# Edge scatter in float32r parts, the loop written out, and new instruction lists for five engines

## The chip, the core and the metric

The kernel runs on one core of a Trainium2 chip. Its engines are TensorE (matmuls and transposes, PE in the profile, with its weight loads as PEld), VectorE (DVE), ScalarE (ACT), GpSimd (POOL) and SyncE (SP), which here issues nearly all DMAs. Each engine runs its own list of instructions in order and waits on semaphores for the others. The metric is the device time of one execution in microseconds; lower is better.

## What is computed

x has 16 batches of 512 nodes by 128 features. Four graph layers follow each other, all within one launch. Layer 0 is eight Euler steps over the adjacency; layer 1 a graph attention with a residual; layer 2 (the "edge" stage) an attention over 256 listed edges; layer 3 a Chebyshev step ("cheb"), a four-head attention of 512 nodes with a mask ("att"), and a feed-forward block with layer norms ("ffn"). The part that the change touches in its arithmetic is the end of the edge layer:

```python
Vt = Xv[:, dst].transpose(1, 0, 2, 3)
Y = jax.ops.segment_sum(attn[..., None] * Vt, src, num_segments=n)
Y = Y.transpose(1, 0, 2, 3).reshape(bt, n, d)
return Y @ W_out.T
```

In the kernel the segment sum is a matmul: U (the 256 edges' weighted values, edges on partitions) times src_rows, a table of zeros and ones with a one where an edge starts at a node.

## The kernel before

`build_front` computes layer 0 for all batches, the tables, and the first two layers' steps for batch 0 and part of batch 1; it ends near 405 us. `build_layers` then runs the other stages as a pipeline over batches. A stage has a lag: `gat` 0, `edge` 1, `cheb` 2, `att` 3, `ffn` 4. `ORDER` (line 1858) holds a list of steps for each engine; in turn i of the loop a step of lag L works on batch i - L, and each "+" behind its name adds one to the lag. `FILL_ORDER` and `DRAIN_ORDER` hold the written-out steps ahead of the loop and behind it, as step:batch. `run` (line 2193) plays the lists: the fill, a hardware loop over i = 6 to 15 (`fori(FILL, B)`), the drain. In the loop, waits for semaphores take values worked out from i in registers, and `wait_alone` (line 157) adds a count of passed waits, `waits_passed`, only there.

The order of work within an engine is thus fixed by the lists alone. The steps that matter:

- `edge_den`, `edge_rden`, `edge_attn`, `edge_u`, `edge_scatter`, `edge_yT`, `edge_out`, `edge_x3`: the chain of the edge layer from the softmax's denominator to its result. `edge_u` (VectorE, line 316) writes U; `edge_scatter` (TensorE, line 378) multiplies it with src_rows in two float32 matmuls.
- `cheb_q`, `cheb_k`: queries and keys, split into high and low parts (`cheb_qsplit`, `cheb_qlow`; `cheb_ksplit`, `cheb_klow`).
- `stack0` to `stack3` (SyncE, line 2234): the parts of one head's queries and keys are copied from SBUF to SBUF into Q_parts and K_parts, four DMAs each, eight for a head. There is one Q_parts and one K_parts for all batches, one slot for each head.
- `att_score0` to `att_score15` (TensorE), `att_mask` (VectorE), `att_exp` (ScalarE), `att_turn` (TensorE), `att_copy` (ScalarE): the sixteen tiles of attention, four for each head; then `att_rows` and `att_pv`, the product with the values. Score j writes bank j modulo 2; mask j writes one of three tiles; exp j one of four.
- `att_score` j with j a multiple of 4 waits for the copies of head j/4 (`parts0` to `parts3` at 128, eight DMAs of 16 each).
- `ffn_turn`, `ffn_x2T`, `ffn_up`, `ffn_gelu`, `ffn_down`: the feed-forward block; GELU needs another table on ScalarE than exp.

What a `stack` waits for stands in these lines: its inputs, and that the scores of the same head of the batch before have been read.

```python
ready_alone(sp, f"{'qk'[which]}_lo", n)
wait_alone(sp, sem("att_score"), n * TILES - TILES + NT * (h + 1), sem("waits_passed"))
```

`stack_head(h)` calls this for the queries, then for the keys. SyncE's loop list before is:

```python
"SP": """
    load_z load_x3+ stack0+ stack2+ store_out+ load_xr stack1+ stack3+ edge_store+ load_x store_v+ cheb_res load_v
""".split(),
```

Of the kernel before, what the change touches and what calls it, by code (L numbers as in the profile page):

```python
# [7 lines left out]
F32 = mybir.dt.float32  # L8
# [8 lines left out]
P = 128  # L17
# [23 lines left out]
def need(eng, sem, value):  # L41
# [11 lines left out]
    gat_eturn gat_eT gat_stat gat_normed gat_T gat_rinv  # L53
# [8 lines left out]
def build(nc, t_in, out):  # L62
    ctx = ExitStack()
    with ctx:
# [41 lines left out]
        src_rows = sb("src_rows", [P, ET, N])  # L106
# [22 lines left out]
        def row4(name, c=NT):  # L129
# [6 lines left out]
                   same_src=same_src, logA=logA, W1ga=W1ga, head_a4=head_a4, G_hi=G_hi, G_lo=G_lo)  # L136
# [59 lines left out]


def edge_stage(nc, k, sem):
# [3 lines left out]
    zT, YT, x2, W = xz, hg, k.gat.x2, k.W  # L202
    b0, b1 = k.bank[4], k.bank[5]
# [19 lines left out]
    def on_gpsimd(pool):  # L223
# [16 lines left out]
        return {"edge_rstd": edge_rstd, "edge_lo": edge_lo}  # L240
# [91 lines left out]
    def on_tensor(pe):  # L332
# [66 lines left out]
def gat_stage(nc, k, sem):  # L399
# [35 lines left out]
    def on_scalar(act):  # L435
# [10 lines left out]
        def gat_exp(n, t):  # L446
            ready(act, "gat_max", n, t + 1, NT)
# [13 lines left out]
    def on_vector(dve):  # L461
# [38 lines left out]
        def gat_max(n, t):  # L500
            nc.vector.scalar_tensor_tensor(g.V[:, t, :], a1[:], small[:, 5, t:t + 1], g.T[:, t, :], ALU.max, ALU.add  # L501
# [73 lines left out]
def build_front(nc, k):  # L575
# [3 lines left out]
    with ExitStack() as c:  # L579
# [41 lines left out]
        gb = [k.src_rows[:].rearrange("p e n -> p (e n)")[:, i * D:(i + 1) * D] for i in range(STEPS)]  # L621
# [150 lines left out]
        def _(pool):  # L772
# [84 lines left out]
            gat["gat_rstd"](1)  # L857

# [969 lines left out]
    "edge": """  # L1828
        edge_lc
# [51 lines left out]
        gat_eT3 cheb_ksplit att_exp12 att_copy10 att_exp13 att_copy11 att_exp14 edge_yT att_copy12 att_exp15
        att_copy13 att_copy14 att_copy15 cheb_vout att_spread
    """.split(),
    "POOL": """
        cheb_rstd gat_rstd edge_rstd ffn_res n2_rstd edge_lo ffn_b2 n1_rstd n3_rstd ffn_x3b n3_g ffn_final
    """.split(),
    "SP": """
        load_z load_x3+ stack0+ stack2+ store_out+ load_xr stack1+ stack3+ edge_store+ load_x store_v+ cheb_res load_v
# [4 lines left out]
        gat_pv0:1 gat_pv1:1 cheb_prop0:0 cheb_prop1:0 cheb_g:0 gat_turn:2 gat_wh:2 gat_s2:2 edge_gather0:1  # L1893
# [904 lines left out]
```

## Time and profile before

| What | Value |
|---|---|
| Median of three runs | 1180.29 us (1178.1 to 1180.65) |
| The profiled execution | 1176.97 us |
| Its span, first to last instruction | 1175.1 us |
| Granted TensorE clock over the span | 0.978 |
| TensorE matmuls | 1097.5 us (93%) |
| VectorE | 852.1 us (73%) |
| ScalarE | 768.5 us (65%) |
| GpSimd | 340.1 us (29%) |

The profile is one execution. Busy time is the union of an engine's instructions; matmuls are pipelined and their ends are modelled, so a row's duration is longer than the distance to the next start, and start-to-start times are the better measure of what a matmul costs. A float32 matmul shows as two records. Waits, register work and DMA issues are not busy time; SyncE's line is made of DMA issues alone, shown as SPq. The loop runs from about 550 to 1000 us; before it stand the front and the fill, after it the drain.

### The profile page before, as it was taken

To read this page: it belongs to the slowest core of one execution; us is meant where nothing else is said; L and a number is where in the kernel's file an instruction comes from. 1 tells how busy PE (TensorE), PEld (TensorE's weight loads), DVE (VectorE), ACT (ScalarE), POOL (GpSimd) and SP (SyncE) were. 2 spreads that over 40 slices of the span, in tenths; PEclk is the share of its full clock that TensorE was granted. 3 is DMA by queue.
4 is the path that set the end of the run, shared out by engine and by line. 5 is a ranking of instruction groups with operands and counts; after the bars stand their busy time and mean duration, and the time that the engine had idled before them with its cause. 6 is when DMAs were issued, how large, how long until landed. Compare 5 with 4: busy or idle time off the path is not lost. (4 is left out here: it accounts for less than half of the span.)

```text
span 1175.1 us, 22865 instructions
## 1 busy us (share of the span) xinstructions
PE 1097.5 (93%) x7105; PEld 873.4 (74%) x7105; DVE 852.1 (73%) x3073; ACT 768.5 (65%) x1640; POOL 340.1 (29%) x465
## 2 busy tenths in 40 slices
PE   7999999999999977999999999999999999999685
PEld 4679899899898856777777777777777777766454
DVE  7774444354364477898898898898898898887655
ACT  4334534432232246898898898898898988987762
POOL 3312104103061012234325325225234244243213
PEclk9999999999999988999999999999999999999887
DMA  3002020021400112424334334334243243243420
GB/s 92 18 11 63 12 79 19 19 81 41 126 10 18 46 47 80 122 66 110 102 89 107 99 98 107 88 104 111 71 116 99 82 122 86 79 113 85 113 64 27
DMA packets 132895, 88.86 MB, mean 76 GB/s; under 512 B 13664, under 2 KB 115424, under 8 KB 132832
## 3 DMA queue, kind: packets, MB, share of 16 engines
q1 hardware_dynamic: 132768, 88.07, 27.6%
q8 instruction: 33, 0.54, 0.2%
q14 instruction: 30, 0.25, 0.1%
q0 software_dynamic: 64, 0.00, 0.0%
HBM read 33.50 MB, written 20.97 MB: 46 GB/s over the span
## 5 line engine op out<-in xcount | busy, mean ns | idle before, releaser
L2453 DVE CUSTOM_DVE_ANT_0 att_Ts<-bank,mask_att 128x512 f32<-128x512 f32 x256 | 174.7, 683 | 64.1 <-PE bank L2608 62.0
L2355 ACT ACTIVATE att_Es<-att_Ts,att_small 128x512 f32<-128x512 f32 x256 | 185.3, 724 | 35.1 <-DVE att_small L2453 34.4
L2662 PE MATMUL bank<-ident,att_Es 128*128 128x128 f32 x1024 | 159.1, 279 | 16.9 <-ACT att_PTs L2364 12.4
L2364 ACT COPY att_PTs<-bank 128x512 f32<-128x512 f32 x248 | 144.0, 581 | 46.2 <-PE bank L2662 45.6
L2662 PEld LDWEIGHTS bank<-ident,att_Es 128*128 128x128 f32 x1024 | 121.8, 143 | 55.3 <-ACT att_PTs L2364 26.0
L2608 PE MATMUL bank<-K_parts,Q_parts 128*128 128x512 f32 x256 | 124.5, 496 | 4.7 <-DMA K_parts<-k_lo 3.2
L2149 POOL TENSOR_SCALAR n_rs<-n_mv 128x4 f32<-128x4 f32 x46 | 13.3, 290 | 309.2 <-DVE n_mv L2144 309.1
L1593 PE MATMUL bank<-G_hi,UT_parts 128*128 128x384 f32 x288 | 77.3, 338 | 1.8 <-DVE G_lo L1436 1.8
L2608 PEld LDWEIGHTS bank<-K_parts,Q_parts 128*128 128x128 f32 x256 | 48.0, 192 | 23.9 <-issue 16.8
L563 PE MATMUL bank<-gat_whs,gat_ETs 128*128 128x128 f32 x512 | 63.8, 280 | 2.0 <-PEq L149 2.0
L563 PEld LDWEIGHTS bank<-gat_whs,gat_ETs 128*128 128x128 f32 x512 | 61.9, 196 | 2.3 <-issue 2.2
L780 POOL TENSOR_SCALAR l_rs<-l_mv 128x4 f32<-128x4 f32 x16 | 3.8, 235 | 197.9 <-DVE l_mv L1060 197.5
L2730 PE MATMUL bank<-att_PTs,v_in 128*32 128x512 f32 x480 | 55.6, 604 | 0.0
L1593 PEld LDWEIGHTS bank<-G_hi,UT_parts 128*128 128x128 f32 x288 | 52.4, 188 | 2.8 <-issue 2.2
L448 ACT ACTIVATE gat_Ts<-gat_Vs,gat_small 128x512 f32<-128x512 f32 x64 | 45.7, 723 | 9.8 <-DVE gat_Vs L501 9.8
L1599 PE MATMUL bank<-Z_hi,P3T_hi 128*128 128x512 f32 x128 | 51.2, 400 | 0.0
L1599 PE MATMUL bank<-Z_hi,P3T_lo 128*128 128x512 f32 x128 | 50.2, 392 | 0.0
L1599 PE MATMUL bank<-Z_lo,P3T_hi 128*128 128x512 f32 x128 | 49.8, 389 | 0.0
L1069 DVE TENSOR_TENSOR UT_parts<-bank,UT_parts 128x512 fp32r<-128x512 f32 x36 | 24.4, 688 | 34.8 <-ACT UT_parts L880 34.6
L2355 ACT ACTIVATION_READ_ACCUMULATOR att_Es<-att_Ts,att_small 128x1 f32 x256 | 49.2, 192 | 0.0
L2151 POOL TENSOR_TENSOR n_rs<-n_rs,neg_half 128x4 f32<-128x4 f32 x46 | 47.8, 1038 | 3.8
L1593 PE MATMUL bank<-G_lo,UT_parts 128*128 128x384 f32 x144 | 48.5, 337 | 0.0
(350 smaller groups left out, 2906.3 us busy)
## 6 DMA issues: line engine op xcount, KB each, us to landing
Q_parts<-q_hi SPq DMA_DIRECT2D x128, 64.0 KB, 2.0
Q_parts<-q_lo SPq DMA_DIRECT2D x128, 64.0 KB, 2.0
K_parts<-k_hi SPq DMA_DIRECT2D x128, 64.0 KB, 2.0
K_parts<-k_lo SPq DMA_DIRECT2D x128, 64.0 KB, 2.0
l_x<-in_x SPq DMA_DIRECT2D x16, 256.0 KB, 2.8
gat_z<-x_after_l SPq DMA_DIRECT2D x16, 256.0 KB, 3.4
gat_xin<-x_after_l SPq DMA_DIRECT2D x16, 256.0 KB, 3.2
x_after_l<-x SPq DMA_DIRECT2D x16, 256.0 KB, 2.4
```

Of the source, the lines that this page charges most:

```text
L448: nc.scalar.activation(g.T[:, t, :], g.V[:, t, :], ACT.Exp, scale=0.8, bias=small[:, 4, t:t + 1], accum_out=small[:, 6, t:t + 1]).then_inc ...
L563: mm = nc.tensor.matmul(a0[:, cols(t)], g.ET[:, s, cols(t)], WhA[:, s, 0:D], start=(s == 0), stop=(s == NT - 1))
L1069: nc.vector.tensor_tensor(UT[:, b % 2, i, 1, :], bank[[6, 4, 5][i]][:], UT[:, b % 2, i, 0, :].bitcast(F32), ALU.subtract).then_inc(sem("ut ...
L1593: mm = nc.tensor.matmul(bank[t][:, 0:BLOCKS * D], left, right[:, i, :], start=(i == 0 and p == 0), stop=(i == BLOCKS - 1 and p == 2))
L1599: mm = nc.tensor.matmul(bank[t][:], left[:, s, cols(t)], right[:, s, :], start=(first and i == 0), stop=(stop and i == 2))
L2151: nc.gpsimd.tensor_tensor(rs[:, 1, :], rs[:, 0, :], k.neg_half[:], ALU.pow).then_inc(sem(tag + "_rs"), 1)
L2355: nc.scalar.activation(att_E[:, j % RING_E, :], att_T[:, j % RING_T, :], ACT.Exp, scale=-1.0, bias=att_small[:, 0, j:j + 1], accum_out=att ...
L2364: nc.scalar.copy(att_PT[:, h, :, cols(q)], c2[:].rearrange("p (s q) -> p s q", q=P)).then_inc(sem("att_pt"), 1)
L2453: nc.vector.tensor_tensor_reduce(att_T[:, j % RING_T, :], [c0, c1][j % 2][:], k.mask_att[:, tile_of(n, j)[1], :], -QK_SCALE, HUGE, ALU.add ...
L2608: return nc.tensor.matmul(dst, left, right, start=True, stop=True)
L2662: mm = nc.tensor.transpose(dst[:, cols(s)], att_E[:, i % RING_E, cols(s)], k.ident[:])
L2730: mm = nc.tensor.matmul(b0[r, :], vD[:, s, r], att_PT[:, h, s, :], start=(s == 0), stop=(s == NT - 1))
```

## The change

Four things:

1. `edge_scatter` takes U in two float32r parts, U_hi and U_lo, four matmuls in one accumulation. A new GpSimd step `edge_parts` makes them from U. src_rows becomes a float32r table; some buffers of the front get rooms of their own.
2. The hardware loop becomes a Python loop, so that all ten turns are in the program with constant wait values. `FILL` is 6, as it was.
3. All lists in `ORDER`, `FILL_ORDER` and `DRAIN_ORDER` are new. The loop's turn begins elsewhere: TensorE's with `att_turn10+` where it began with `att_score0`.
4. Waits that the old lists implied, or that held for the last batch alone, are written for every batch: `att_mask` waits for `att_exp`, every score waits for `att_T`, and `gat_exp0` and `gat_max0` wait for `gat_small`.

```diff
+        def edge_parts(n):
+            ready_alone(pool, "edge_u", n)
+            nc.gpsimd.tensor_copy(U_hi[:], U[:]).then_inc(sem("edge_uhi"), 1)
+            ready(pool, "edge_uhi", n)
+            nc.gpsimd.tensor_tensor(U_lo[:], U[:], U_hi[:].bitcast(F32), ALU.subtract).then_inc(sem("edge_ulo"), 1)
...
         def edge_scatter(n):
-            ready(pe, "edge_u", n)
+            ready(pe, "edge_ulo", n)
             for e in range(ET):
-                mm = nc.tensor.matmul(b0[:], U[:, cols(e)], k.src_rows[:, e, :], start=(e == 0),
-                                      stop=(e == ET - 1))
+                for i, part in enumerate([U_hi, U_lo]):
+                    mm = nc.tensor.matmul(b0[:], part[:, cols(e)], k.src_rows[:, e, :],
+                                          start=(e == 0 and i == 0), stop=(e == ET - 1 and i == 1))
             mm.then_inc(sem("edge_scattered"), 1)
...
 ORDER = {
     "PE": """
-        att_score0 att_score1 att_turn15+ att_rows+ att_pv0+ att_pv1+ att_score2 gat_turn att_turn0 att_score3 ffn_wo
-        cheb_prop0 att_turn1 att_score4 cheb_prop1 gat_wh cheb_g gat_s2 att_turn2 att_score5 ffn_turn att_turn3
-        ffn_up0 att_score6 ffn_up1 att_turn4 att_score7 ffn_down0 ffn_down1 cheb_x1turn att_turn5 att_score8
-        edge_gather0 att_turn6 edge_gather1 att_score9 cheb_q edge_x att_turn7 att_score10 gat_eturn0 edge_lcol
-        edge_lb0 edge_lb1 gat_eturn1 att_turn8 att_score11 cheb_k gat_eturn2 gat_eturn3 att_turn9 att_score12 edge_v
-        edge_den att_turn10 att_score13 gat_pv0 att_turn11 att_score14 edge_scatter att_turn12 att_score15 edge_out
-        att_turn13 gat_pv1 att_turn14 cheb_v
+        att_turn10+ gat_pv0+ att_turn11+ att_score15+ edge_scatter+ att_turn12+ gat_pv1+ att_turn13+ edge_out+
+        att_score0 att_turn14+ cheb_v+ att_score1 att_turn15+ att_rows+ att_pv0+ att_pv1+ att_score2 att_turn0
+        att_score3 gat_turn ffn_wo cheb_prop0 att_score4 cheb_prop1 gat_wh att_turn1 cheb_g att_score5 att_score6
+        ffn_turn att_turn2 att_score7 ffn_up0 ffn_up1 gat_s2 att_turn3 ffn_down0 att_turn4 ffn_down1 cheb_x1turn
+        att_score8 att_turn5 edge_gather0 att_score9 edge_gather1 att_turn6 cheb_q edge_x att_score10 att_score11
+        att_turn7 edge_lcol gat_eturn0 gat_eturn1 edge_lb0 edge_lb1 cheb_k att_turn8 gat_eturn2 att_score12
+        att_score13 att_turn9 gat_eturn3 edge_v edge_den att_score14
...
     "DVE": """
...
+        edge_le+ att_mask12+ gat_stats edge_rden+ edge_attn+ edge_u+ att_mask13+ cheb_klow+ att_mask14+ gat_aggr
+        n3_stats+ att_mask15+ n3_aggr+ n3_apply+ att_rv+ edge_x3+ gat_rinv+ cheb_stats cheb_aggr att_mask0 att_mask1
+        gat_x2a+ gat_x2b+ edge_stats edge_aggr gat_apply att_scale cheb_lo att_mask2 ffn_y2 n2_stats att_mask3 n2_aggr
...
     "ACT": """
...
+        att_exp3 gat_wh_out0 att_copy1 gat_wh_out1 att_exp4 ffn_x2T att_copy2 edge_hi ffn_gelu0 ffn_gelu1 att_copy3
...
     "POOL": """
-        cheb_rstd gat_rstd edge_rstd ffn_res n2_rstd edge_lo ffn_b2 n1_rstd n3_rstd ffn_x3b n3_g ffn_final
+        edge_parts+ n3_rstd+ ffn_res n3_g+ cheb_rstd gat_rstd ffn_final+ edge_rstd n2_rstd n1_rstd edge_lo ffn_b2
+        ffn_x3b
     """.split(),
     "SP": """
-        load_z load_x3+ stack0+ stack2+ store_out+ load_xr stack1+ stack3+ edge_store+ load_x store_v+ cheb_res load_v
+        load_x3++ stack3++ edge_store+++ stack0++ store_v++ stack1++ load_v+ store_out++ load_x+ cheb_res++ load_xr
+        load_z stack2++
     """.split(),
 }
 FILL_ORDER = {
...
     "SP": """
...
+        load_z:2 stack0:0 load_z:3 stack2:0 stack1:0 load_x:2 edge_store:0 edge_store:1 store_v:0 stack3:0 cheb_res:0
+        load_x:3 load_z:4 load_xr:0 load_v:0 stack1:1 stack3:1 stack2:1 stack0:1 cheb_res:1 load_z:5 store_v:1
+        load_v:1 load_x:4 load_xr:1
...
 DRAIN_ORDER = {
...
     "SP": """
...
+        load_x3:10 edge_store:12 stack0:12 stack1:12 load_x3:11 stack3:12 cheb_res:12 store_out:10 store_v:12
+        stack2:12 stack0:13 load_v:12 edge_store:13 load_xr:12 stack2:13 stack1:13 load_x:15 load_x3:12 cheb_res:13
+        store_v:13 store_out:11 stack3:13 cheb_res:14 edge_store:14 stack0:14 load_v:13 load_xr:13 stack1:14
+        store_v:14 load_xr:14 stack3:14 stack2:14 load_x3:13 store_out:12 load_v:14 stack1:15 cheb_res:15 stack0:15
+        stack3:15 stack2:15 load_xr:15 edge_store:15 store_v:15 load_v:15 store_out:13 load_x3:14 store_out:14
+        load_x3:15 store_out_0:15 store_out_1:15
...
             listed(FILL_ORDER[engine])
-            with fori(FILL, B) as i:
+            for i in range(FILL, B):
                 iteration(i)
...
             def att_mask(n, j):
-                if last(n):
-                    need(dve, sem("att_exp"), n * TILES + j + 1 - RING_T)
+                need(dve, sem("att_exp"), n * TILES + j + 1 - RING_T)
...
             def att_score(n, j):
...
-                if j in (2, 3) or last(n):
-                    need(pe, sem("att_T"), n * TILES + j - 1)
+                need(pe, sem("att_T"), n * TILES + j - 1)
```

## Rows read from the trace of the kernel before

**Rows 1.** The page, section 1: busy us (share of the span) xinstructions.
```profile
PE 1097.5 (93%) x7105; PEld 873.4 (74%) x7105; DVE 852.1 (73%) x3073; ACT 768.5 (65%) x1640; POOL 340.1 (29%) x465
```

**Rows 2.** Busy time by engine in one period; clock, DMA share, GB/s.
```profile
700.46:745.69 45.23, 43.70 (x325) 34.02 (x323) 40.41 (x159) 39.51 (x90) 16.22 (x22) 1.00 0.36 99
```

**Rows 3.** TensorE's waits from 600 to 1000 us: total, times, longest.
```profile
PE bank L2753 <- ACT ffn_mT L2348: 7.8, 8, 1.0
```

**Rows 4.** SyncE's timeline: start us, us, what.
```profile
709.49 1.14 SPq L2244 DMA_DIRECT2D Q_parts<-q_hi  x2
710.68 1.22 SPq L2244 DMA_DIRECT2D Q_parts<-q_lo  x2
712.08 0.51 SPq L2244 DMA_DIRECT2D K_parts<-k_hi  x1
...
713.90 0.59 SPq L2244 DMA_DIRECT2D K_parts<-k_lo  x1
...
727.63 0.41 SPq L2219 DMA_DIRECT2D x_after_l<-x  x1
```

**Rows 5.** Busy time by engine, in straight code and in the drain.
```profile
100.00:200.00 100.00, 100.00 (x500) 88.42 (x499) 44.17 (x121) 43.49 (x72) 18.50 (x27) 1.00 0.12 35
1100.00:1150.00 50.00, 37.59 (x269) 25.67 (x268) 28.31 (x87) 31.08 (x70) 10.25 (x10) 0.84 0.27 70
```

**Rows 6.** TensorE's timeline in one turn: start us, us, what.
```profile
708.12 1.88 PE L381 MATMUL bank<-src_rows,edge_us 128*128 128x512 f32 x4
709.83 0.60 PE L2662 MATMUL bank<-ident,att_Es 128*128 128x128 f32 x4
710.19 0.48 PE L2608 MATMUL bank<-K_parts,Q_parts 128*128 128x512 f32 x1
710.68 1.16 PE L388 MATMUL bank<-w_WoutT,edge_hgs 128*128 128x128 f32 x8
711.68 0.60 PE L2662 MATMUL bank<-ident,att_Es 128*128 128x128 f32 x4
712.12 1.95 PE L563 MATMUL bank<-gat_whs,gat_ETs 128*128 128x128 f32 x16
713.90 0.60 PE L2662 MATMUL bank<-ident,att_Es 128*128 128x128 f32 x4
```

**Rows 7.** TensorE's timeline at the gather, the same columns.
```profile
737.97 0.39 PE L339 MATMUL bank<-edge_pick,h_hi 128*128 128x512 f32 x1
738.20 0.40 PE L339 MATMUL bank<-edge_pick,h_lo 128*128 128x512 f32 x1
```

**Rows 8.** Timelines of VectorE and GpSimd, 705 to 709 us.
```profile
707.18 0.42 DVE L318 TENSOR_TENSOR edge_us<-bank,edge_small 128x256 f32<-128x256 f32 x1
...
707.18 1.28 POOL L2314 TENSOR_TENSOR ffn_x<-ffn_x,rowv 128x512 f32<-128x512 f32 x1
```

**Rows 9.** The line that issues Q_parts and K_parts: duration ns min/median/max.
```profile
L2244 SPq DMA_DIRECT2D K_parts<-k_hi x128: 507/534/1488, 436.8 to 1116.7; - x128
L2244 SPq DMA_DIRECT2D K_parts<-k_lo x128: 580/591/1637, 437.3 to 1117.3; - x128
...
DMA to landing us min/median/max: 1.9/2.0/3.2
```

**Rows 10.** TensorE's timeline; in brackets idle time before, and its end.
```profile
406.69 4.54 PE L563 MATMUL bank<-gat_whs,gat_ETs 128*128 128x128 f32 x24 [2.01 <-PEq L149]
...
424.60 0.79 PE L339 MATMUL bank<-edge_pick,h_hi 128*128 128x512 f32 x1 [2.96 <-POOL h_lo L237]
```

**Rows 11.** Busy time by engine just after these two gaps; clock.
```profile
424.00:427.00 3.00, 2.40 (x6) 1.92 (x7) 2.93 (x12) 0.00 (x0) 0.54 (x1) 0.50 0.30 88
430.00:433.00 3.00, 2.74 (x14) 1.72 (x14) 1.32 (x4) 2.37 (x7) 0.00 (x0) 0.88 0.00 0
407.00:410.00 3.00, 3.00 (x16) 3.00 (x16) 0.98 (x8) 0.00 (x0) 1.70 (x4) 0.50 0.61 180
410.00:413.00 3.00, 2.13 (x18) 1.94 (x17) 0.63 (x2) 2.27 (x5) 0.00 (x1) 0.96 0.00 0
```

More of the change, by code:

```diff
@@ L1908 @@
-        gat_eturn3:4 edge_v:3 edge_den:3 att_turn9:1 att_score12:1 cheb_k:2 att_turn10:1 att_score13:1 edge_scatter:3
-        att_turn11:1 cheb_v:2 att_score14:1 edge_out:3 att_turn12:1 att_score15:1 gat_pv0:4 att_turn13:1 gat_pv1:4
-        att_turn14:1 att_score0:2 att_score1:2 att_turn15:1 att_rows:1 att_pv0:1 att_pv1:1 att_score2:2 cheb_prop0:3
-        ffn_wo:1 gat_turn:5 att_turn0:2 cheb_prop1:3 att_score3:2 att_turn1:2 gat_wh:5 cheb_g:3 att_score4:2
-        ffn_turn:1 att_turn2:2 gat_s2:5 ffn_up0:1 att_score5:2 ffn_up1:1 att_turn3:2 att_score6:2 ffn_down0:1
@@ new lines @@
+        edge_gather1:1 edge_x:1 cheb_x1turn:0 edge_lcol:1 edge_lb0:1 cheb_q:0 gat_eturn0:2 edge_lb1:1 gat_eturn1:2
+        gat_eturn2:2 cheb_k:0 gat_eturn3:2 edge_v:1 edge_den:1 cheb_v:0 gat_pv0:2 edge_scatter:1 att_score0:0
+        att_score1:0 edge_out:1 gat_pv1:2 att_turn0:0 att_score2:0 att_score3:0 att_turn1:0 att_score4:0 gat_turn:3
+        att_score5:0 gat_wh:3 att_score6:0 att_turn2:0 gat_s2:3 cheb_prop0:1 cheb_prop1:1 att_score7:0 att_score8:0
+        att_turn3:0 cheb_g:1 edge_gather0:2 att_score9:0 att_turn4:0 edge_gather1:2 gat_eturn0:3 att_turn5:0
@@ new lines @@
+        edge_scatter:3 att_turn11:1 cheb_v:2 gat_eturn3:4 edge_out:3 att_turn12:1 gat_pv0:4 att_turn13:1 gat_pv1:4
+        att_turn14:1 att_score0:2 att_score1:2 att_turn15:1 att_rows:1 att_pv0:1 att_pv1:1 cheb_prop0:3 ffn_wo:1
+        att_score2:2 att_turn0:2 cheb_prop1:3 att_turn1:2 gat_turn:5 att_score3:2 att_score4:2 cheb_g:3 gat_wh:5
+        att_turn2:2 att_score5:2 ffn_turn:1 gat_s2:5 att_turn3:2 ffn_up0:1 att_score6:2 att_turn4:2 att_score7:2
+        ffn_up1:1 ffn_down0:1 ffn_down1:1 att_score8:2 att_score9:2 att_turn5:2 edge_gather0:4 edge_gather1:4
@@ new lines @@
+        gat_max0:3 gat_row2:3 gat_max1:3 gat_row3:3 cheb_y:1 att_mask7:0 n1_stats:1 att_mask8:0 n1_aggr:1 att_mask9:0
+        n1_apply:1 edge_z:2 cheb_x1:1 gat_max2:3 edge_lc:2 att_mask10:0 gat_max3:3 att_mask11:0 edge_max0:2
+        edge_max1:2 cheb_qlow:1 edge_max2:2 edge_max3:2 edge_le:2 att_mask12:0 gat_rinv:3 att_mask13:0 edge_rden:2
+        edge_attn:2 edge_u:2 cheb_klow:1 gat_stats:4 gat_aggr:4 att_mask14:0 att_mask15:0 edge_x3:2 att_rv:0
+        att_mask0:1 cheb_stats:2 cheb_aggr:2 gat_x2a:3 att_mask1:1 gat_x2b:3 gat_apply:4 edge_stats:3 edge_aggr:3
@@ L1976 @@
+        ffn_res:0 edge_lo:2 n1_rstd:1 edge_parts:2 gat_rstd:4 cheb_rstd:2 edge_rstd:3 n2_rstd:0 edge_lo:3 ffn_b2:0
+        n1_rstd:2 edge_parts:3 gat_rstd:5 ffn_res:1 cheb_rstd:3 n3_rstd:0 edge_rstd:4 n3_g:0 n2_rstd:1 ffn_x3b:0
+        ffn_final:0 n1_rstd:3 edge_lo:4 ffn_b2:1 ffn_x3b:1
     """.split(),
     "SP": """
-        load_z:2 edge_store:0 cheb_res:0 load_x:2 load_z:3 stack0:0 stack2:0 edge_store:1 stack1:0 load_x:3 stack3:0
-        store_v:0 cheb_res:1 load_v:0 load_xr:0 stack0:1 load_x3:0 load_z:4 stack2:1 edge_store:2 stack1:1 load_x:4
@@ L1980 @@
-        stack3:1 store_v:1 load_z:5 cheb_res:2 load_v:1 stack0:2 store_out:0 load_xr:1 stack2:2 stack1:2 edge_store:3
-        stack3:2 load_x:5 store_v:2 load_v:2 cheb_res:3
+        load_z:2 stack0:0 load_z:3 stack2:0 stack1:0 load_x:2 edge_store:0 edge_store:1 store_v:0 stack3:0 cheb_res:0
+        load_x:3 load_z:4 load_xr:0 load_v:0 stack1:1 stack3:1 stack2:1 stack0:1 cheb_res:1 load_z:5 store_v:1
+        load_v:1 load_x:4 load_xr:1
     """.split(),
@@ L2058 @@
     """.split(),
 }
-FILL = 1 + max(LAG[STAGE_OF[step.rstrip("+")]] + step.count("+") for order in ORDER.values() for step in order)
+FILL = 6
 def build_layers(nc, k):
```

313 lines of the change are left out of this document (153 added, 160 removed).

## The prediction, made before the change was run

> **What bounds the kernel now.** I read the page first: TensorE is busy for 93% of the span [rows 1]. The table by stage says where the rest is. From about 550 to 1000 us the kernel repeats itself every 45.23 us (one batch of each stage, ten turns of the loop), and in one such period TensorE is busy 43.70 us, VectorE 40.41, ScalarE 39.51, GpSimd 16.22 [rows 2]. So TensorE sets the period, and VectorE and ScalarE are only 5 to 6 us behind it. Of the 1.5 us that it is idle, 1.0 us lies ahead of `ffn_down0`, eight times in the 400 us asked for, with GELU's output as what ended it [rows 3]. Start-to-start times in the timeline show as much again hidden under the modelled ends (steps that last longer than the same step elsewhere in the period), so some 3.1 us a period, an estimate, is loss by order, not work. The third thing to read is SyncE's own line, because the change re-orders it: every copy of `stack` is a separate DMA issue, and the issues of one head follow each other at 0.55 to 0.63 us [rows 4]. The straight-line stages at the ends (fill and drain) are looser: TensorE is busy 37.59 of 50 us from 1100 to 1150 us, at 0.84 of its clock [rows 5].
>
> **The scatter itself.** Before, `edge_scatter` is two float32 matmuls of 512 columns, four records from 708.12 to the next start at 709.83, so 1.71 us [rows 6]. After, it is four float32r matmuls. The nearest rows are those of `edge_gather`, the same shape and types, 0.23 us from start to start [rows 7]: 4 x 0.23 = 0.92 us. That saves 0.8 us a batch, 16 x 0.8 = 12.8 us at most, if TensorE is what waits for nobody.
>
> **The new link through GpSimd.** `edge_parts` stands between `edge_u` and `edge_scatter`: a cast and a subtraction on 128x256. GpSimd's 128x512 tensor operation took 1.28 us and VectorE's `edge_u` 0.42 us [rows 8]. I take half of 1.28 for each of the two, plus 0.2 us for the hand-overs: 1.5 us. The bounds are 0.7 us (the half-sized pair at a third of that) and 2.8 us (no saving by size). The new VectorE list runs `edge_rden`, `edge_attn`, `edge_u` back to back, so U is ready some 1.1 us after `edge_den`; before, `cheb_klow` and `att_mask13` stood between. TensorE has 3.1 us of other work between `edge_den` and the scatter. So the link is hidden, with half a microsecond to spare. If it is late by 1 us, that is 1 us of TensorE a batch, but in the loop it is swallowed by the wait below, which starts with score 15, ahead of the scatter.
>
> **The order of TensorE, VectorE and ScalarE.** Scores may now run up to three tiles ahead of their transposes, each with its waits written out (`att_T`, `att_exp`). These waits carry ordering that the old list gave by itself; I cost them at nothing, since a satisfied wait shows as no gap. `ffn_down0` now has `gat_s2` and `att_turn3` ahead of it and ScalarE runs `ffn_x2T`, one copy, `edge_hi` and GELU in a row, so the 1.0 us stall shrinks rather than goes: 1.28 us of table load and two GELUs still stand there. Of the 3.1 us I take half as won back, 1.5 us; bounds 0 and 3.1 us.
>
> **The loop written out.** The register arithmetic and the counting of passed waits go. None of it is on TensorE's path now. Straight-line code of the same density already runs with TensorE 100.00 us busy in 100 [rows 5], so I cost the longer program at nothing; a bound for it is in the rivals.
>
> **SyncE's list, which decides.** In the new loop list the copies of head 3 stand ahead of those of head 0: `stack3++ edge_store+++ stack0++ store_v++ stack1++ ... stack2++`, all four of the same batch n. `stack` for head h of batch n waits until the scores of head h of batch n-1 are read. For head 3 that is all sixteen. SyncE issues in order, so head 0's copies, which `att_score0` of batch n needs, can't start until score 15 of batch n-1 is done and head 3's eight DMAs have been issued. In the old list `stack0+` came first, behind score 3 only, and its query half was issued long before. The chain, from the start of score 15:
> score 15 itself 0.48 us [rows 6]; a wait and the eight issues of head 3, 9.49 to 14.49 us in the old trace, 5.0 us, plus 0.2; the store of x3 0.5 (0.41 alone, 0.6 in a row of issues); head 0 from its first to its last issue 4.4 us [rows 4]; landing 2.0 us, in the range 1.9 to 3.2 [rows 9]. Sum: 0.48 + 5.2 + 0.5 + 0.1 + 4.4 + 2.0 = 12.7 us. What TensorE does meanwhile: score 15 0.32, scatter 0.92, turn 12 0.36, `gat_pv1` 1.78, turn 13 0.36, `edge_out` 1.00 [rows 6] = 4.8 us. It then stands before `att_score0` for 12.7 - 4.8 = 7.9 us, in every turn. Behind `att_score0` on TensorE are turn 14, `cheb_v`, score 1, turn 15 and the value products; VectorE waits for it in `att_mask0` and ScalarE in `att_copy14`. The time cannot be made up, since the chain starts again with the next score 15.
>
> **The clock after the stall.** After gaps of 2.01 and 2.96 us on TensorE [rows 10] the granted clock was at 0.50, 1.2 GHz, until 3.6 and 6.1 us after work had begun again (0.50 in 407:410, 0.96 in 410:413; 0.50 in 424:427, 0.88 in 430:433) [rows 11]. At 1.2 GHz a microsecond does half its work, so these cost 1.8 and 3.1 us. A gap of 7.9 us is longer than both and should do it every time; I take 3.0, with 1.8 below and 4.0 above. The Trainium skill, page "TensorE: Matmul & The Clock Gate", Part 1, says that an idle array falls back to the half rate by default and that activity releases it; it speaks against this change, and the trace agrees.
>
> **Sum.** A turn: 45.2 - 0.8 - 1.5 + 7.9 + 3.0 = 53.8 us, 8.6 more than now; ten turns, 86 us. Fill: batch 1 has its heads in the order 1, 3, 2, 0, so three groups (5.2 + 5.2 + 4.4) and the landing stand between score 15 of batch 0 and `att_score0`, 17.5 us against 5.6 us of work: 11.9 + 3 of clock, less 0.8 for the scatter and some 4 us of old fill gaps closed, so +10 (0 to +16). Drain: `load_x` of batch 15 stands behind `stack0`, `stack2` and `stack1` of batch 13, and VectorE needs it before `att_mask1`, some 6 us; batch 15 needs head 2 last of four groups for its third score, some 4 us net; clock 3; less 1.6 for scatters and 3 for order: +8 (0 to +16). The profiled execution took 1176.97 us: 1176.97 + 86 + 10 + 8 = 1281. The median of the runs, 1180.29, is 3 us above it, so 1284.
>
> **Rivals.** *The stall without the clock.* Everything as above, but the clock is back at once: -3.0 a turn and -6 at the ends, 1284 - 36 = 1248. With all 3.1 us of order won back as well and the ends at nothing it is 1284 - 30 - 16 - 18 = 1220, the low end.
> *SyncE's issues don't hold TensorE: faster.* This needs 16 issues and a landing to fit in TensorE's 4.8 us: 0.48 + 0.3 + 2.0 + 16d < 4.8 gives d below 0.13 us an issue. Then the scatter (0.8) and the order (1.5) are won: 1180 - 23 - 7 at the ends = 1150. Against it are 512 issues in the old trace at medians of 0.53 to 0.59 us, in the written-out fill (from 436.8 us) as in the loop [rows 9].
> The Trainium skill, page "DMA: Bandwidth & Descriptors", section "Anatomy of one DMA", has descriptor generation as small and says that many can be emitted before it shows; going by that this rival would be the outcome, but the issues in this trace do not bear it out.
> *The program becomes too long to load in time.* A few of SyncE's issues took up to 1.5 and 1.6 us in place of 0.6 (the maxima of [rows 9]), which may be such loading; these numbers don't say. If each engine lost 1 us a turn to that, +10 on top: 1294. The busy 100 us of straight code [rows 5] speaks against more.
> *The edit doesn't do what it says* (TensorE takes the four passes at the old rate): 4 x 0.43 in place of 0.92, no gain, +0.8 a batch: 1292 in the main case.
>
> **Chances.** Main case 0.65 (1284); stall without the clock loss 0.14 (1248); loading or no gain in the passes 0.12 (1293); issues hidden 0.09, of which about 0.08 ends faster by over 0.2% (1150) and 0.01 within 0.2%, which is about what a measurement of this kernel can tell from none. So 0.91 slower. The range must reach over the stall without the clock and over a longer clock loss (4.0 us a turn, +10) with slower landings (+1.2 a turn, +12): 1230 to 1312.
>
> **What would show it.** In the new trace the longest wait of TensorE should be `att_score0` (line of `one`) ended by the DMA of K_parts, near 8 us, ten times or more, with the granted clock below 1.0 in every turn; SyncE's line should show sixteen issues in a row after score 15; the scatter should be 4 records 0.23 us apart, GpSimd's two operations near 0.65 us. The period is read from one `att_score0` to the next: 53.8 us if I am right, 51 with no clock loss, 43 if the issues are hidden. The forecast is wrong if K_parts ends no wait in the loop.

## The result, and the profile after

| kernel | median us | lowest to highest | profiled execution us | its span us | mean clock |
|---|---|---|---|---|---|
| before | 1179.19 | 1175.63 to 1180.65 | 1176.97 | 1175.1 | 0.978 |
| changed | 1323.35 | 1319.43 to 1327.7 | 1325.99 | 1323.8 | 0.925 |

The changed kernel is slower: 1.1239 times the time before, 95% interval 1.1211 to 1.1268, +144 us. I had forecast +104 us and at most +132. The direction and the main mechanism were right, and the size was too small.

The page of the changed kernel first (busy time with its share; then the span in 40 slices, TensorE's busy share and its clock in tenths):

```profile
span 1323.8 us, 21440 instructions
...
PE 1122.5 (85%) x7105; PEld 902.7 (68%) x7105; DVE 885.6 (67%) x3073; ACT 764.7 (58%) x1640; POOL 362.5 (27%) x497
...
PE   8999999999997595877978779787787879968866
...
PEclk9999999999998797988989889898898989988978
```

TensorE was busy for 93% of the span before [rows 1], now for 85%, and from slice 14 on the clock drops again and again. What ended TensorE's waits from 520 to 1080 us (total, times, longest):

```profile
PE bank L2631 <- DMA K_parts<-k_lo: 77.2, 11, 8.9
PE bank L2621 <- DVE cheb_x1s L2464: 12.3, 8, 2.3
PE bank L2775 <- ACT ffn_mT L2372: 6.8, 10, 0.8
```

The first row is the wait that I had forecast (line 2631 is `one`, which issues the scores): nine of its eleven waits stand ahead of `att_score0`, of batches 3 to 11, 7.7 to 8.9 us each, where I had named ten or more. Another of 4.4 us stands ahead of head 2's first score of batch 2. The third answers to [rows 3]: `ffn_down0` still waits for GELU, 0.7 us a time in place of 1.0. The second row has no counterpart in the kernel before, and I had not foreseen it.

TensorE's timeline in one turn (start, length, line, operation; in brackets the idle time before it and what ended it):

```profile
885.94 0.48 PE L2631 MATMUL bank<-K_parts,Q_parts 128*128 128x512 f32 x1
886.25 0.39 PE L394 MATMUL bank<-src_rows,edge_uhi 128*128 128x512 f32 x1
...
887.18 0.60 PE L2684 MATMUL bank<-ident,att_Es 128*128 128x128 f32 x4
...
889.83 1.06 PE L401 MATMUL bank<-w_WoutT,edge_hgs 128*128 128x128 f32 x8
898.59 0.80 PE L2631 MATMUL bank<-K_parts,Q_parts 128*128 128x512 f32 x1 [7.70 <-DMA K_parts<-k_lo]
```

and SyncE's at the same time:

```profile
886.49 1.14 SPq L2268 DMA_DIRECT2D Q_parts<-q_hi  x2
887.68 1.22 SPq L2268 DMA_DIRECT2D Q_parts<-q_lo  x2
...
891.48 0.58 SPq L2243 DMA_DIRECT2D x_after_l<-x  x1
892.16 1.14 SPq L2268 DMA_DIRECT2D Q_parts<-q_hi  x2
...
896.51 0.59 SPq L2268 DMA_DIRECT2D K_parts<-k_lo  x1
902.66 0.37 SPq L2251 DMA_DIRECT2D values<-v_out  x1
```

Score 15 starts at 885.94. SyncE's eight copies of head 3 begin when it ends (886.49), the x3 store follows at 891.48, head 0's eight copies at 892.16, and the last of them is issued at 896.51. `att_score0` starts 2.1 us later: 12.65 us after score 15, where I had worked out 12.7. The four passes of the scatter take 0.93 us (886.25 to 887.18) against 1.71 [rows 6].

The granted clock just after this gap (stretch, its length, busy us of the five engines, then PEclk):

```profile
898.00:901.00 3.00, 2.42 (x10) 2.24 (x11) 0.70 (x2) 0.59 (x1) 2.71 (x4) 0.50 0.01 3
901.00:904.00 3.00, 3.00 (x46) 2.62 (x49) 1.48 (x6) 1.55 (x3) 0.00 (x0) 0.72 0.15 45
904.00:910.00 6.00, 6.00 (x56) 3.22 (x45) 4.48 (x18) 5.90 (x16) 1.85 (x4) 1.00 0.43 111
```

Below, "the period" is the mean of the eight turns from the first score of batch 3 to that of batch 11. Before, these start at 579.0 and 941.3 us, 45.3 us a turn; in the changed kernel at 624.6 and 1065.4, 55.1 us. The span grew by 148.7 us: 94 in the ten turns from batch 2 to batch 12 (453.1 to 547.4), 26 between the first scores of batch 0 and batch 2 (92.8 to 118.5), 23 from that of batch 12 to the end (188.5 to 211.8), and 5 ahead of batch 0. The last figure I don't explain: with the same front part, the first score started between 438.9 and 448.5 us in the profiles of this study, and between 442.5 and 448.5 in those whose code up to there is the changed kernel's.

### The profile page after: what moved, and what is told of

Its sections match the earlier page's. It is cut to its first block, busy times and chain, and to the rows that moved or that the text cites. A ratio compares the mean times of both kernels' runs of the same rounds, so it can differ in the third digit from the quotient of the medians.

```text
span 1323.8 us, 21440 instructions
## 1 busy us (share of the span) xinstructions
PE 1122.5 (85%) x7105; PEld 902.7 (68%) x7105; DVE 885.6 (67%) x3073; ACT 764.7 (58%) x1640; POOL 362.5 (27%) x497
## 4 chain that ended last, share of the span: by engine, by line
PE 29%; DVE 14%; SPq 13%; issue 5%; DMA 3%; ACT 2%; POOL 1%; POOLq 0%; DVEq 0%; ACTq 0%
SPq L2268 12%; PE bank L2631 7%; PE bank L2684 5%; PE bank L2752 4%; DMA K_parts<-k_lo 2%; PE bank L2627 2%; PE bank L580 2%; DVE att_Ts L2476 2%; DVE cheb_y L2214 2%; PE bank L572 2%; DVE n_stat L2161 1%; PE bank L351 1%; DVE gat_Ts L497 1%; PE bank L372 1%; DVE cheb_y L2206 1%
## 5 line engine op out<-in xcount | busy, mean ns | idle before, releaser
L2684 PE MATMUL bank<-ident,att_Es 128*128 128x128 f32 x1024 | 166.3, 289 | 11.2 <-ACT att_PTs L2388 9.3
L2684 PEld LDWEIGHTS bank<-ident,att_Es 128*128 128x128 f32 x1024 | 130.7, 149 | 49.0 <-ACT att_PTs L2388 22.4
L2631 PEld LDWEIGHTS bank<-K_parts,Q_parts 128*128 128x128 f32 x256 | 50.2, 208 | 148.7 <-DMA K_parts<-k_lo 107.4
L248 POOL CAST edge_uhi<-edge_us 128x256 fp32r<-128x256 f32 x16 | 6.4, 398 | 215.4 <-DVE edge_us L330 215.4
```

The costliest lines, as they stand in the source:

```text
L2631: return nc.tensor.matmul(dst, left, right, start=True, stop=True)
L2684: mm = nc.tensor.transpose(dst[:, cols(s)], att_E[:, i % RING_E, cols(s)], k.ident[:])
```

## The experiments

The theory was that SyncE's order makes the stall and that the stall makes the clock loss. Its rivals were the written-out loop, the scatter with its link through GpSimd, and the new compute lists. The runs fall into three groups by when they ran, and the kernel before, measured beside each group, had a median of 1175.72 us for the first four runs below, 1178.95 for four others (the fill, the drain, GpSimd's order in the kernel before, and the old scatter in the new order) and 1176.01 for the rest. A difference of 3 us between runs of different groups is therefore not safe.

**SyncE's three lists mended, all else as changed.**

```diff
-        load_x3++ stack3++ edge_store+++ stack0++ store_v++ stack1++ load_v+ store_out++ load_x+ cheb_res++ load_xr
-        load_z stack2++
+        stack0++ stack1++ stack2++ stack3++ store_v++ edge_store++ load_x+ load_xr load_v+ load_z
+        store_out++ load_x3+ cheb_res+
```

(fill and drain alike: stores and loads ahead of the copies that they stood behind; some stores and loads also change their lag by a turn.)

> The changed kernel with SyncE's three lists (fill, loop, drain) re-ordered by when each item can start: the copies of heads 0, 1, 2, 3 in that order, the x3 store and the z, x and residual loads ahead of the copies that they stood behind; all other engines' lists stay the changed ones. Theory (SyncE's order is the cause): the wait of TensorE for K_parts ahead of att_score0 goes in all ten turns, and the half-clock stretch after it; the period falls from 54.7 by 8.4 of stall and 2.5 of clock to about 44 us, the fill loses its 13.5 and 10.3 us gaps, the drain its 8.1 us gap: 1323 - 107 - 30 - 12 = about 1175 us, between 1160 and 1200. Rival (the new compute lists or the GpSimd link are themselves slower than the old ones): the K_parts wait goes, but other waits take its place and the time stays above 1220 us with a period above 47 us.

Measured: 1188.69 us (1181.01 to 1191.14), 1.0119 of before [1.0085, 1.0153]; the period is 46.05 us (569.9 to 938.3). So about 135 of the 144 us were SyncE's order. But the kernel is not faster than before, and the time is 14 us above what I expected. From 520 to 1080 us K_parts ends a single wait of 1.9 us. What is left is another one:

```profile
PE bank L2621 <- DVE cheb_x1s L2464: 17.9, 10, 2.4
```

**One exchange in SyncE's loop list.**

```diff
-        load_x3++ stack3++ edge_store+++ stack0++ store_v++ stack1++ load_v+ ...
+        load_x3++ stack0++ edge_store+++ stack3++ store_v++ stack1++ load_v+ ...
```

> The changed kernel with one exchange in SyncE's loop list: head 0's copies where head 3's stood and head 3's where head 0's stood. Theory: stall and clock loss ahead of att_score0 go in the ten turns, and the ends stay as they are: 1323 - 10 x 10.9 = about 1214 us (1205 to 1250; the upper part if head 1's copies, which now stand behind head 3's, come late for score 4). Rival (the stall has another cause, for example the compute order): the time stays within 30 us of 1323.

Measured: 1234.36 us (1230.55 to 1238.68). Two words exchanged give back 89 us, with a period of 45.5 us (610.1 to 973.9). The wait for cheb_x1s is there too, 15.2 us in ten turns, and in both runs one for gat_z, 5.6 us in ten turns. They are of the size of the 14 to 20 us by which this run and the one before came out above my figures.

**The same move in the kernel before.** Its loop was written out, and `stack3+` put ahead of `stack0+`.

```diff
-        load_z load_x3+ stack0+ stack2+ store_out+ load_xr stack1+ stack3+ edge_store+ load_x ...
+        load_z load_x3+ stack3+ stack0+ stack2+ store_out+ load_xr stack1+ edge_store+ load_x ...
```

> The kernel before with its loop written out and only one move: in SyncE's loop list head 3's copies ahead of head 0's; nothing else of the change. Theory: head 0's copies start after score 15 and head 3's eight issues, 0.5 + 5.2 + 4.4 + 2.0 = 12.1 us, against some 5 us of TensorE's work: a stall of about 7 us with K_parts as its end, 2.5 us of half clock, less the 2 to 3 us of slack that the old period has: +7 a turn in ten turns, about 1250 us (1230 to 1280). Rival (the issues are hidden, or the slowdown belongs to the other lists): no more than 5 us from the same kernel without the move.

Measured: 1274.21 us (1271.45 to 1276.03), 1.0839 [1.0804, 1.0874]. The period is 55.1 us (585.4 to 1026.0): ten turns of 10 us. The gaps on TensorE are 6.85 to 8.04 us, all ended by K_parts. The cause brings the effect in a kernel that has none of the other parts but the written-out loop, which by the next run costs nothing. I had taken 2 to 3 us a turn off for slack in the old order; none of that came.

**The loop written out alone.** `with fori(FILL, B) as i:` becomes `for i in range(FILL, B):` in the kernel before.

> The kernel before with its loop written out and nothing else. Theory: TensorE does not wait for register work, so the same time within 3 us. Rival (a longer program is loaded late): 10 us or more above the kernel before, spread over the ten turns.

Measured: 1174.6 us (1172.06 to 1179.79), ratio 0.9983 [0.9959, 1.0007], period 45.1 us. The loading of a longer program is out as a cause: the interval leaves it 1 us at most.

**The clock alone.** Idle time of TensorE filled in the changed kernel:

```diff
+                need(pe, sem("att_T"), n * TILES + j - 1)
+                if j == 0 and 3 <= n <= 12:
+                    for r in range(32):
+                        one(c0[:], k.src_rows[:, 0, 0:P], k.src_rows[:, 0, :])
                 if t == 0:
                     ready(pe, f"parts{h}", n, 128, 128)
-                need(pe, sem("att_T"), n * TILES + j - 1)
```

> The changed kernel with 32 rounded-type matmuls of 512 columns (0.23 us each, 7.4 us) put between att_score0's wait for bank c0 and its wait for K_parts, for batches 3 to 12; they write into the bank that the score overwrites, and the copies of K_parts are as late as before. Theory (a part of each turn's loss is the half clock after the stall): the granted clock stays at 1.0 through the loop, the stall is filled, and the period falls from 54.7 by 2 to 3 us, 1323 - 25 = about 1298 us (1293 to 1305). Rival (the half clock is hidden under other waits): within 5 us of 1323.

Measured: 1309.82 us (1305.83 to 1314.2), 13.5 less. The same turn without the extra matmuls, then with them:

```profile
734.40:789.10 54.70, 44.65 (x323) 35.72 (x323) 42.92 (x158) 39.00 (x88) 17.48 (x24) 0.91 0.30 82
```

```profile
732.70:785.10 52.40, 49.77 (x354) 39.75 (x354) 42.91 (x158) 39.07 (x88) 17.43 (x23) 1.00 0.32 86
```

The granted clock is at 1.00 throughout, and the period falls from 55.1 to 52.8 us: 2.35 us a turn is what the half clock costs. Eight turns give 19 us; batch 12, which has the extra matmuls but no stall to hide them in, gives 5.3 back (46.6 to 51.9 us). That makes the 13.5, about, and my total had forgotten batch 12.

**The fill and the drain, each alone.** Only that one of SyncE's lists is mended in the changed kernel.

> The changed kernel with SyncE's fill list alone re-ordered (x3 store of batch 0 and load_z of batch 3 ahead of the copies of batch 0, heads 0, 1, 2, 3 in order for batches 0 and 1); loop and drain lists as changed. Between the first scores of batch 0 and batch 2 the changed kernel took 118.5 us, the run with all SyncE's lists mended 84.3, and its first score came 5 us earlier. Theory (all of that is SyncE's fill list, and the loop that follows loses as before): 1323 - 36 = about 1287 us (1280 to 1298). Rival (the fill's part is 10 us, as I had forecast, and the rest of the loss belongs to VectorE's and TensorE's own fill lists): about 1313 us.

> The changed kernel with SyncE's drain list alone re-ordered (load_x of batch 15 ahead of the copies of batch 13, head 0 or 1 first, head 3 last). From the first score of batch 12 to the end the changed kernel took 211.8 us, the run with all SyncE's lists mended 194.6. Theory: 1323 - 17 = about 1306 us (1300 to 1312). Rival (the drain's loss is in the other engines' lists): within 5 us of 1323.

Measured: 1288.35 us (1285.54 to 1296.7) with the fill list mended, 35 less; 1301.1 us (1298.24 to 1308.28) with the drain list mended, 22 less. So the two ends held 57 us of SyncE's share. Loop, fill and drain one by one give 89 + 35 + 22 = 146 us, mended together 135.

What stood behind them in the changed kernel: VectorE's waits from 440 to 520 us, then from 1160 to 1221 us.

```profile
DVE x L338 <- DMA x_after_l<-x: 9.0, 1, 9.0
DVE gat_stat L480 <- DMA gat_z<-x_after_l: 5.2, 1, 5.2
```

```profile
DVE x L533 <- DMA gat_xin<-x_after_l: 8.9, 1, 8.9
```

In the fill the x3 store of batch 0 stands behind three heads' copies of batch 0, so `edge_x3:1` waits 9.0 us, `att_mask2:0` stands behind it on VectorE, and TensorE stands 10.3 us. In the drain `load_x:15` is issued behind the copies of batch 13, and TensorE stands 8.15 us.

**GpSimd's order.** The new wait for cheb_x1s needed a cause. VectorE and GpSimd in one turn of the run with SyncE's lists mended:

```profile
635.45 3.09 DVE L2214 SCALAR_TENSOR_TENSOR cheb_y<-cheb_y,n_rs,rowv 128x128 f32<-128x128 f32 x4
...
639.07 1.26 DVE L2464 SCALAR_TENSOR_TENSOR cheb_x1s<-cheb_y,cheb_hs 128x512 f32<-128x512 f32 x1
```

```profile
634.31 1.04 POOL L2175 TENSOR_TENSOR n_rs<-n_rs,neg_half 128x4 f32<-128x4 f32 x1
635.32 1.27 POOL L243 TENSOR_TENSOR h_lo<-edge_hs,h_hi 128x512 fp32r<-128x512 f32 x1
636.54 1.32 POOL L2330 TENSOR_TENSOR ffn_y2s<-ffn_y2s,rowv 128x512 f32<-128x512 f32 x1
```

The four pieces of `n1_apply` take 3.09 us in place of 1.13 (see below), and they stretch just while GpSimd runs `edge_lo` and `ffn_b2`. The changed GpSimd list puts these two directly behind `n1_rstd`, which releases `n1_apply`: the collision is built in. So the list was re-ordered, in the kernel with SyncE's lists mended:

```diff
-        edge_parts+ n3_rstd+ ffn_res n3_g+ cheb_rstd gat_rstd ffn_final+ edge_rstd n2_rstd n1_rstd edge_lo ffn_b2
-        ffn_x3b
+        edge_parts+ n3_rstd+ n3_g+ cheb_rstd gat_rstd edge_rstd ffn_res ffn_final+ n2_rstd ffn_b2 edge_lo n1_rstd
+        ffn_x3b
```

> The run with SyncE's lists mended, and GpSimd's loop list re-ordered besides: ffn_res behind n3_g, edge_rstd ahead of ffn_final, ffn_b2 and edge_lo ahead of n1_rstd; nothing else. In the run with SyncE's lists mended, VectorE's cheb_y of line 2214 took 855 ns a piece against 347 in the kernel before, gat_z 559 against 343, ffn_y3s 574 against 359, cheb_x1s 942 against 686, each time beside a GpSimd operation of 1.27 us on 128x512 that its own GpSimd link had released a moment before; and TensorE waits 17.9 us in ten turns for cheb_x1s. Theory (GpSimd work placed beside VectorE's two-input operations stretches them, and in x1's case TensorE waits for it): the four means fall back to within 50 ns of the kernel before, TensorE's wait for cheb_x1s falls from 1.8 to under 0.5 us a turn, the period from 46.2 to about 44.5 us, 1189 - 15 = about 1174 us. Rival (VectorE's order alone makes cheb_x1 late): the means fall, the wait for cheb_x1s stays above 1.2 us a turn and the time stays within 4 us of 1189.

Measured: 1158.75 us (1157.62 to 1160.5), 0.9853 of before [0.9822, 0.9885]: faster than both kernels. The period is 43.8 us (571.5 to 921.8). The same step of VectorE, and the group of it over 450 us:

```profile
635.10 1.13 DVE L2214 SCALAR_TENSOR_TENSOR cheb_y<-cheb_y,n_rs,rowv 128x128 f32<-128x128 f32 x4
```

```profile
L2214 DVE SCALAR_TENSOR_TENSOR cheb_y<-cheb_y,n_rs,rowv 128x128 f32<-128x128 f32 x40 | 12.4, 370 | 0.0
```

370 ns a piece against 855; gat_z fell from 559 to 340, ffn_y3s from 574 to 343, cheb_x1s from 942 to 684. On TensorE the wait for cheb_x1s fell from 17.9 us to 1.2, and that for gat_z, 5.6 us, is gone: 22.3 us together, and the period's 2.25 us a turn make 22. I had left gat_z out, and the gain of 30 us is twice what I expected. The spans of the two profiled executions differ by 22.8 us; that of the run with only SyncE mended was the fastest of its five, 7.7 us below their median, and what makes the others longer no trace shows. The collision is not wholly gone: the first pass of cheb_y (line 2206) now takes up to 919 ns, with a mean of 483 against 348.

**GpSimd's order in the kernel before.** Loop written out, and `n1_rstd` moved ahead of two steps:

```diff
-        ... ffn_res n2_rstd edge_lo ffn_b2 n1_rstd n3_rstd ffn_x3b n3_g ffn_final
+        ... ffn_res n2_rstd n1_rstd edge_lo ffn_b2 n3_rstd ffn_x3b n3_g ffn_final
```

> The kernel before with its loop written out, and in GpSimd's loop list n1_rstd moved ahead of edge_lo and ffn_b2, so that these two run while VectorE applies n1; nothing else. Theory (a GpSimd operation on 128x512 beside a two-input operation of VectorE stretches it): cheb_y's second pass goes from 347 to 700 ns or more a piece, 1.5 to 2 us a turn on VectorE, of which TensorE sees 0.5 to 2 as a wait for cheb_x1s: 1175 + 10 = about 1185 us (1178 to 1195). Rival (the stretch came from the new VectorE list): the mean stays at 347 ns, the time within 3 us of 1175.

Measured: 1191.63 us (1189.49 to 1194.49), 1.0104 [1.0072, 1.0136], period 46.8 us against 45.1. The group that took 347 ns a piece before, and TensorE's new wait:

```profile
L2190 DVE SCALAR_TENSOR_TENSOR cheb_y<-cheb_y,n_rs,rowv 128x128 f32<-128x128 f32 x40 | 28.9, 781 | 0.0
```

```profile
PE bank L2598 <- DVE cheb_x1s L2440: 8.6, 9, 1.0
```

The stretch follows GpSimd's order, in a kernel with the old VectorE list. Of the 1.7 us a turn, 1.0 stands as this wait; the rest I did not follow.

**VectorE's wait for n3.** On top of the 1158.75 us kernel, `n3_apply+` moves behind `cheb_aggr`, and GpSimd's `gat_rstd cheb_rstd` go ahead of `n3_g+`.

> As the run before, and VectorE's n3_apply moved behind cheb_aggr, GpSimd's n3_g behind cheb_rstd and gat_rstd ahead of cheb_rstd. VectorE waits 14.7 us in ten turns for n3's rstd with n3_apply directly behind n3_aggr. Theory (VectorE is off TensorE's path there): that wait goes, and the time is within 4 us of the run with GpSimd's order mended. Rival (VectorE's 1.5 us a turn is on the path): another 8 to 15 us less.

Measured: 1166.81 us (1164.43 to 1168.85), 8 us more; neither theory. The old wait goes, and a longer one stands in its place:

```profile
DVE att_small L2549 <- ACT att_Es L2379: 19.5, 10, 2.1
```

`att_rv` now comes first and waits for ScalarE's last exponentials, 1.95 us a turn in place of 1.47. The wait for n3's rstd seems to have been time in which those finished. `ffn_y2` waits for GpSimd's `ffn_res` (0.8 a turn) as it did in the run before, and TensorE now waits for ffn_y2s every turn (0.5). The period is 44.25 us against 43.8, 4.5 of the 8 us; that these waits make it is my reading, and no run isolates them.

**The scatter, from two sides.** First the changed kernel with all old lists (and `edge_parts` put in):

> The changed kernel with all lists of all engines (fill, loop, drain) put back to those of the kernel before; edge_parts goes into GpSimd's list behind n3_rstd, and edge_u directly behind edge_attn so that it is in time. What is left of the change is the scatter in four passes, its link through GpSimd, the written-out loop and the added waits. Theory: the scatter wins 0.8 us a batch where TensorE waits for nobody, 1176 - 13 = about 1163 us, up to 1172 if edge_parts comes late. Rival (the link through GpSimd or the added waits cost more than the passes save): above 1180 us, with TensorE waiting for edge_ulo.

Measured: 1178.85 us (1177.88 to 1182.65), ratio 1.003 [1.001, 1.0049], period 45.05 us. No gain, and not by the wait that the rival named: edge_ulo ends only two short waits. What the added waits cost by themselves no run shows. TensorE's timeline suggests where the gain went:

```profile
709.00 0.48 PE L2626 MATMUL bank<-K_parts,Q_parts 128*128 128x512 f32 x1
709.46 0.50 PE L394 MATMUL bank<-src_rows,edge_uhi 128*128 128x512 f32 x1
...
710.48 0.60 PE L2679 MATMUL bank<-ident,att_Es 128*128 128x128 f32 x4
...
711.71 1.16 PE L401 MATMUL bank<-w_WoutT,edge_hgs 128*128 128x128 f32 x8 [0.39 <-ACT edge_hgs L279]
```

The passes are shorter by 0.7 us (709.46 to 710.48 against 1.71 before [rows 6]). But `edge_out` follows with only a turn and a score between, and waits 0.39 us for ScalarE's `edge_yT`. From score 14 to `edge_out` it is 2.71 us here and was 2.88 before, so at most 0.2 us of the 0.7 is left there. The new TensorE list has `gat_pv1` and two turns between the two. So the second run puts the old scatter back into the 1158.75 us kernel:

```diff
-            ready(pe, "edge_ulo", n)
+            ready(pe, "edge_u", n)
             for e in range(ET):
-                for i, part in enumerate([U_hi, U_lo]):
-                    mm = nc.tensor.matmul(b0[:], part[:, cols(e)], k.src_rows[:, e, :],
-                                          start=(e == 0 and i == 0), stop=(e == ET - 1 and i == 1))
+                mm = nc.tensor.matmul(b0[:], U[:, cols(e)], k.src_rows[:, e, :].bitcast(F32), start=(e == 0),
+                                      stop=(e == ET - 1))
```

> The kernel of the run with SyncE's lists mended and GpSimd's loop list re-ordered (1158.75 us), with the scatter put back to two float32 matmuls on U as in the kernel before, and no edge_parts. Theory (there TensorE waits for nobody around the scatter): 0.8 us a batch come back, 1159 + 13 = about 1171 us. Rival (as with the old lists, where the passes were shorter by 0.8 us and the period by 0.1: what follows the scatter waits for other engines): within 4 us of 1159.

Measured: 1167.85 us (1163.9 to 1169.9), 9 us more; the period is 44.4 us (577.7 to 932.6) against 43.8. Here 0.6 of the 0.8 us a turn seems to reach the end. But the two runs are of different groups: each against the kernel before beside it, they are at 0.9897 [0.9865, 0.9929] and 0.9853 [0.9822, 0.9885], which makes 5 us rather than 9, with intervals that overlap, and the periods come from one profile each. So the scatter pays some 5 to 9 us in the new lists, near the edge of what these runs can tell, and nothing in the old ones. That it is TensorE's order which makes the difference is not shown, since all engines' lists differ between the two pairs.

## Why the prediction was wrong in size

A turn, in the terms of my sum, each with what the runs gave (periods of the runs above):

| term | forecast | measured | from |
|---|---|---|---|
| period before | 45.2 | 45.3 | |
| scatter | -0.8 | -0.6 | 44.4 to 43.8, old scatter against new |
| order of TensorE, VectorE, ScalarE | -1.5 | -0.9 | 45.3 to 43.8, less the scatter (a remainder, with SyncE's and GpSimd's lists mended) |
| GpSimd beside VectorE | not seen | +2.25 | 43.8 to 46.05 |
| gap ahead of `att_score0` | +7.9 | +8.0 | nine gaps, 7.7 to 8.9 |
| not explained by the rows above and below (a remainder) | | -1.3 | 55.1 - 46.05 - 8.0 - 2.35 |
| clock | +3.0 | +2.35 | 55.1 to 52.8 |
| sum | 53.8 | 55.1 | |

- *What bounds the kernel, and SyncE's list:* right. The gap is where I put it, ended by what I named, and 8.0 us long against 7.9. Moved into the old kernel it makes +100 us alone.
- *The clock:* the mechanism was right (with the array kept busy the clock stays at 1.00), the price 2.35 us in place of 3.0. In the turn shown, the half clock lasted until between 901 and 904 us, some 3 to 5 us after work had begun again at 898.6. The 0.72 over 901 to 904 puts it near 902.7, 4.1 us after. That is nearer to my lower gap of [rows 10], with its 3.6 us, than to the upper.
- *The order of the compute lists:* the sign was right, the size 0.9 of 1.5. My wrong step was to cost the new GpSimd list by its waits alone ("hidden, with half a microsecond to spare" for `edge_parts`, which holds: 0.40 and 0.73 us, and it hardly ends a wait). I never asked what the steps that move beside VectorE's work do to it, though GpSimd's list was part of the diff. That is +2.25 us a turn. In the changed kernel part of it does not show: the wait for gat_z is not among TensorE's waits there, and that for cheb_x1s is 1.5 us a time in place of 1.8, together some 0.8 us of the remainder of 1.3. With the run of one exchange (period 45.5) as the base in place of the 46.05, the remainder is 0.75.
- *The fill:* forecast +10 (0 to +16), measured +26 between batches 0 and 2, and 35 us given back by that list alone. The stall ahead of batch 1 was there as forecast (13.5 us against 11.9, as the key half of head 1's copies, too, was issued only after score 15 had started). What I missed is the other consumer of SyncE's order: I followed the copies to TensorE, but not the x3 store and `load_z` that stand behind them to VectorE. That was a second gap of 10.3 us with its own stretch of half clock (0.54 over 455 to 470 us).
- *The drain:* forecast +8 (0 to +16), measured +23, 22 given back. I had named `load_x:15` at 6 us; the wait was 8.9 us on VectorE and 8.15 on TensorE. For batch 15 I had put 4 us net, and TensorE waited 4.2 us ahead of its first score and 5.1 ahead of its third. The 4.6 us that I took off for scatters and order did not come: with SyncE's drain list mended, the stretch from batch 12's first score to the end still takes 191.0 us, against 188.5 before.
- *The sum:* the ten turns came to 94 us against 86. The two ends came to 49 us against 18, and another 5 stand ahead of batch 0. The failed step is the terms of the two ends, with their bounds: the fill's was taken from one stall where there were two, and the drain's two stalls were sized short and had 4.6 us of gains set against them. Each end came out above its bound of 16 us.
- *The rivals:* the stall without the clock fell with the run that filled the idle array. Program loading fell with the written-out loop alone. "No gain in the passes" is wrong as I meant it (the records are 0.23 us apart), but with the old lists the shorter passes bring nothing to the end. "SyncE's issues don't hold TensorE" fell in the trace: 0.53 to 0.63 us each, sixteen of them after score 15 with only the x3 store between. The Trainium skill, page "DMA: Bandwidth & Descriptors", section "Anatomy of one DMA", which I had set beside that rival, describes the path from GpSimd, where it has descriptor generation as small. The copies here come from SyncE, so it did not bear on them, and no run here tests it.
- *Slips in the sums:* the rival without a gain in the passes counts ten batches; sixteen make 1297 us in place of 1292. The sum of 1220 that I called the low end lies below the range, whose low end is 1230. The terms of the fill's chain, with score 15 itself, add up to 17.3 us, not 17.5. None of them changes the account.

## What to carry to other kernels

In an in-order queue the place of a DMA is a dependency: of every step that is moved, follow each transfer behind it to its own consumer, in the fill and drain lists too. Ask of every GpSimd step not only what waits for it but what VectorE runs beside it: large GpSimd operations belong ahead of the small ones that release VectorE, not behind them. A shorter pass need not pay: look at whether its successor's other inputs are early. Here the same scatter was worth nothing in one order and some 5 to 9 us in another.

## What the runs showed of the hardware that I had not expected

Some of VectorE's operations seem to stand still beside GpSimd, and the means hide it. Pieces of `cheb_y` (128x128, two inputs in SBUF) that take 347 ns took 855 on the mean, and 781 in the old kernel with the loop written out and GpSimd's order changed; `gat_z` and `ffn_y3s` (tensor_scalar, one tensor input in SBUF) went from 343 to 559 and from 359 to 574. The single pieces have two lengths (run with SyncE's lists mended, 560 to 1010 us; duration ns min/median/max):

```profile
L2214 DVE SCALAR_TENSOR_TENSOR cheb_y<-cheb_y,n_rs,rowv x40: 338/1279/1359, 590.0 to 1008.4; 128x128 f32<-128x128 f32 x40
L491 DVE TENSOR_SCALAR gat_z<-gat_z,gat_mv,gat_rs x40: 332/335/1239, 576.3 to 992.5; 128x128 f32<-128x128 f32 x40
```

17 of the 40 pieces of `cheb_y` overlap no 128x512 operation of GpSimd and take 0.34 us; the 23 that do take 1.24 us on the mean, about as long as GpSimd's operation itself (1.27 to 1.32 us). In the turn shown above, two such pieces and two of 0.34 us make the 3.09 us. Of `gat_z` and `ffn_y3s` it is one piece in four. Other operations are untouched: in the kernel before, 21 masks, which read a bank, lay wholly beside such an operation and took 0.68 us as elsewhere, and so did the statistics of `cheb_y` (one input in SBUF), 0.28 us.

The Trainium skill names this on the page "GPSIMD Engine Reference", section "Specifications": the SBUF interfaces are shared with VectorE, with contention for VectorE instructions in a 2-port mode or with two SBUF inputs. The rows of `cheb_y` agree; `gat_z` and `ffn_y3s` have one tensor input in SBUF, and no run here shows whether they ran in a 2-port mode.

TensorE kept its full clock through 52 us turns when rounded-type matmuls of 0.23 us filled the gap, though they did no useful work; left idle for 7.7 us, it ran the next score in 0.80 us in place of 0.48, at a granted clock of 0.50.
